# Layer 0's decay matrices by scans on VectorE, with G in two PSUM banks and D times x added by VectorE

## The reference

```python
dt = softplus(zxbcdt[..., D_INNER + CONV_DIM:] + dt_bias)
dA = jnp.exp(dt * A)
dBx = jnp.einsum('blhp,bln,blh->blhpn', x, Bmat, dt)
def step(state, inp):
    dA_t, dBx_t = inp
    state = state * dA_t[:, :, None, None] + dBx_t
    return (state, state)
y = jnp.einsum('lbhpn,bln->blhp', states, Cmat)
y = y + D[None, None, :, None] * x
y = rmsnorm(y.reshape(B, L, D_INNER) * silu(z), norm_gate_w, eps=1e-05)
return y @ W_out
```

## Time and profile before

| | us |
|---|---|
| three runs | 1697.21, 1696.18, 1690.65 |
| median | 1696.18 |
| the profiled execution | 1692.49 |
| its span, from first to last instruction | 1690.8 |
| busy in the span: TensorE / VectorE / ScalarE / GpSimd | 1556.4 / 1122.5 / 768.9 / 706.8 |
| mean granted TensorE clock | 0.954 of 2.4 GHz |

### The profile page before, as it was taken

How to read it: one execution, slowest core, us unless ns; L and a number is a source line. 1 busy time by engine, 2 the same in 40 slices (tenths; PEclk the granted TensorE clock), 3 DMA queues, 4 the chain that set the end, 5 groups by cost and what they waited for, 6 DMA issues and landing times.

```text
span 1690.8 us, 23271 instructions
## 1 busy us (share of the span) xinstructions
PE 1556.4 (92%) x7307; PEld 1073.6 (63%) x7307; DVE 1122.5 (66%) x2583; ACT 768.9 (45%) x1562; POOL 706.8 (42%) x751
## 2 busy tenths in 40 slices
PE   4989999999999999999878888899988999999996
PEld 3555756757566575756554455555557888988985
DVE  4868577684866758576248888987875654555542
ACT  1425162451625425162316555566545555555562
POOL 1555536364563655536311222233232553443452
PEclk7979989999999999999889999999999999999998
DMA  6000020101001010010122111111102442433432
GB/s 200 0 13 13 1 63 1 50 12 38 25 0 59 4 50 12 0 51 1 38 88 90 35 63 62 60 58 52 50 25 85 102 100 65 85 74 86 96 51 25
DMA packets 66855, 84.00 MB, mean 50 GB/s; under 512 B 12360, under 2 KB 57296, under 8 KB 66768
## 3 DMA queue, kind: packets, MB, share of 16 engines
q1 hardware_dynamic: 54480, 65.86, 12.1%
q0 software_dynamic: 12288, 17.05, 6.0%
HBM read 57.53 MB, written 25.36 MB: 49 GB/s over the span
## 4 chain that ended last, share of the span: by engine, by line
PE 26%; issue 13%; POOL 7%; DVE 3%; ACT 1%; DMA 1%; PEldq 0%; POOLq 0%; DVEq 0%; PEld 0%; SPq 0%
PE bank L2060 25%; POOL yb L920 2%; POOL Xs L912 2%; POOL ry L928 1%; PE bank L2435 1%; DVE am L1874 1%; POOL out L976 1%; POOL ry L925 0%; POOL xg L951 0%; DVE hits L1780 0%; DVE E L1896 0%; DVE yb L1907 0%; DVE u L1874 0%; DMA xg<-rows_d,IDX 0%; DMA hT<-xnT_d 0%
## 5 line engine op out<-in xcount | busy, mean ns | idle before, releaser
L2015 DVE TENSOR_TENSOR aml<-m0big,amh 128x512 fp32r<-128x512 f32 x128 | 88.0, 688 | 175.4 <-ACT amh L1320 175.3
L976 POOL DMA_INDIRECT out<-EW,IDX x64 | 105.1, 1642 | 223.5 <-DVE EW L2000 208.9
L1315 ACT ACTIVATE m0big<-bank,eb 128x512 f32<-128x512 f32 x128 | 87.9, 687 | 161.3 <-PE bank L2060 145.9
L2060 PE MATMUL bank<-w2h,amh 128*128 128x256 f32 x512 | 147.9, 289 | 0.0
L2060 PE MATMUL bank<-h2T,EW 128*128 128x512 f32 x320 | 146.8, 596 | 0.3
L2060 PE MATMUL bank<-w2h,aml 128*128 128x256 f32 x512 | 144.8, 283 | 0.0
L2060 PE MATMUL bank<-w2l,amh 128*128 128x256 f32 x512 | 144.7, 283 | 0.0
L2060 PEld LDWEIGHTS bank<-Xdt,E 128*128 128x128 f32 x768 | 95.7, 201 | 56.7 <-issue 56.7
L2060 PE MATMUL bank<-EW,am 128*128 128x256 f32 x512 | 115.8, 379 | 1.2 <-DVE am L1639 1.2
L920 POOL TENSOR_TENSOR yb<-yb,zs 128x512 f32<-128x512 f32 x32 | 40.5, 1267 | 171.9 <-DVE yb L1911 171.8
L1110 ACT ACTIVATE am<-bank,b 128x512 f32<-128x512 f32 x64 | 43.9, 686 | 148.0 <-PE bank L2060 148.0
(11 more groups left out here) (327 smaller groups left out, 3810.0 us busy)
## 6 DMA issues: line engine op xcount, KB each, us to landing
EW<-in_e_w SPq DMA_DIRECT2D x16, 1024.0 KB, 5.5
m0big<-dA_d SPq DMA_DIRECT2D x16, 512.0 KB, 4.7
xin<-in_L_attn_x SPq DMA_DIRECT2D x8, 512.0 KB
xp<-in_L_attn_x SPq DMA_DIRECT2D x8, 512.0 KB, 3.7
rows_d<-xo SPq DMA_DIRECT2D x8, 512.0 KB, 3.0
x_d<-xb SPq DMA_DIRECT2D x8, 512.0 KB, 4.0
xnT_d<-nT SPq DMA_DIRECT2D x8, 512.0 KB, 4.4
out<-x SPq DMA_DIRECT2D x32, 128.0 KB, 1.7
```

Of the source, the lines that this page charges most:

```text
L976: g.indirect_dma_start(out=out_rows, out_offset=bass.IndirectOffsetOnAxis(ap=IDX[:, 4 * u + c:4 * u + c + 1], axis=0), in_=ye[:, q, c, :], ...
L1315: a.activation(am2[:, j % 2, :], bank[j % 2][:, :], ACT.Gelu, bias=eb1[:, u // 2, j:j + 1]).then_inc(gelu_sig.sem, 1)
L2015: v.tensor_tensor(aml[:, j % 4, :], am2[:, j % 2, :], amh[:, j % 4, :], ALU.subtract).then_inc(am_low.sem, 1)
L2060: return t.matmul(out_, lhsT, rhs, start=first, stop=last)
```

## The change

It concerns layer 0 alone. R, its two sums on TensorE per chunk, ScalarE's exps of them and the mask product Gm are removed. In their place:

- TensorE transposes the log decays of the step (LOGT, 32 rows: four chunks of eight heads), behind the decay sums, and both now stand behind the input projections. ScalarE takes the exp into dAT0, whose first column is zero.
- SP stores dAT0 to DRAM and loads it back broadcast to 128 partitions, one transfer of 512 KB per chunk, into four buffers E0 (two new ones and the two halves of E). SP's loop over the steps is written out.
- VectorE scans each buffer in place in two halves against four identities side by side (ID0, in the room of b2), `scans`. The scans of chunks 0 and 1 stand around `chunk(0)`, those of chunk c+2 behind `sums(c)` and `mixed0(c-1)`.
- G and B's transposes go to two banks in turn, MISC and the former SEG; VectorE multiplies the scanned decays with G straight from PSUM.
- VectorE adds XD to yb in `sums`, in place of GpSimd in `gated`; GpSimd's XD waits for the sum two chunks back.

```diff
-        R = sb("R", [P, 8 * P])
+        dA0b = sb("dA0b", [P, 8 * P])
+        dAT0 = sb("dAT0", [CH * 8, P])
...
+        E0 = (dA0a[:, :], dA0b[:, :], E[:, 0, :], E[:, 1, :])
...
+        LOGT = MISC[0:CH * 8, 384:512]
+        GP0 = (MISC[:, 128:256], SEG[:, 128:256])
+        BTP0 = (MISC[:, 256:320], SEG[:, 256:320])
+        ID0 = b2[:, :, :].rearrange("p a n -> p (a n)")
...
+            def store_decays(i):
+                sp.wait_ge(own, 2)
+                s0.dA.wait_ge(sp, i, 1)
+                for c in range(CH):
+                    s0.dA_loaded[c].wait_ge(sp, i, 0)
+                sp.dma_start(dA0_d.rearrange("c (h t) -> (c h) t", t=P), dAT0[:, :]).then_inc(s0.dA_stored.sem, 16)
+            def load_decays0(i, c):
+                if c == 0:
+                    s0.dA_stored.wait_ge(sp, i, 16)
+                s0.intra_full.wait_ge(sp, i - 1, c + 1)
+                sp.dma_start(E0[c], dA0_d[c].partition_broadcast(P)).then_inc(s0.dA_loaded[c].sem, 16)
+            def decays_of(i):
+                store_decays(i)
+                load_decays0(i, 0)
+                load_decays0(i, 1)
+            def later_decays_of(i):
+                load_decays0(i, 2)
+                load_decays0(i, 3)
...
-            with sp.Fori(1, STEPS - 2) as b:
+            for b in range(1, STEPS - 2):
                 load_x(b + 2)
+                decays_of(b + 1)
                 load_residual(b + 1)
+                later_decays_of(b + 1)
                 store_back(b)
...
-            def terms(L, s, i, c, ch):
-                s.a.wait_ge(pool, i, 1)
-                s.seg_full.wait_ge(pool, i, c * L.segs)
-                nh = L.heads
-                v = R[:, 0:nh * P].rearrange("p (h t) -> p h t", h=nh)
-                a = s.dtv_buf[:, 1, c * nh:(c + 1) * nh].unsqueeze(2).to_broadcast([P, nh, P])
-                g.tensor_tensor(v, triU[:, :].unsqueeze(1).to_broadcast([P, nh, P]), a,
-                                ALU.mult).then_inc(s.R.sem, 1)
...
+                s.y0.wait_ge(pool, i, c - 1)
...
                 s.y0.wait_ge(pool, i, c + 1)
-                s.xd.wait_ge(pool, i, c + 1)
-                ch.put(g.tensor_tensor(yb[:, q, :], yb[:, q, :], XD[:, q, :], ALU.add))
-                ch.see(pool)
                 s.zs.wait_ge(pool, i, c + 1)
                 g.tensor_tensor(yb[:, q, :], yb[:, q, :], zs[:, q, :], ALU.mult).then_inc(s.yg.sem, 1)
...
-                if f is not None:
-                    terms(L, s, f, 0, pool0)
                 if b is not None:
                     back_rms(b, CH - 1, CH, poolb)
                     h2_sig.wait_ge(pool, b, CH)
...
-                    terms(L, s, f, 1, pool0)
                     xrows(L, s, f, 0)
                     xrows(L, s, f, 1)
                     for c in range(CH):
-                        if c + 2 < CH:
-                            terms(L, s, f, c + 2, pool0)
                         gated(L, s, f, c, pool0)
...
                 s.cum_full.wait_ge(act, i, 1)
                 a.activation(s.ex_buf[:, :, 0:n], CUM.rearrange("p (j n) -> p j n", j=3)[:, :, 0:n],
                              ACT.Exp).then_inc(s.ex.sem, 1)
+                s.dA_stored.wait_ge(act, i, 0)
+                a.activation(dAT0[:, 1:P], LOGT[:, 1:P], ACT.Exp).then_inc(s.dA.sem, 1)
...
                     if j == 0:
                         raw(L, s, i, 4)
+                        decay_exp(L, s, i)
...
-                def decays(j):
-                    s.seg_full.wait_ge(act, i, c * L.segs + j + 1)
-                    a.activation(E[:, q, 512 * j:512 * (j + 1)], SEG[:, :], ACT.Exp).then_inc(s.E.sem, 1)
-                s.intra_full.wait_ge(act, i, c - 1)
-                decays(0)
                 p = front_wait(act, L, s, i, f"xt{c}")
                 s.xdt.wait_ge(act, i, c - 1)
                 s.xd.wait_ge(act, i, c - 1)
                 a.activation(Xsb[:, q, :], p[:, :], ACT.Copy).then_inc(s.xsb.sem, 1)
-                for j in range(1, L.segs):
-                    decays(j)
...
                 if f is not None:
-                    decay_exp(L, s, f)
                     chunk(L, s, f, 0)
...
-                v.tensor_tensor(Gm[:, q, :], GP, triU[:, :], ALU.mult).then_inc(s.gm.sem, 1)
...
-                v.tensor_copy(Bs[:, q, 0:L.state], BTP[:, 0:L.state]).then_inc(s.bs.sem, 1)
+                v.tensor_copy(Bs[:, q, 0:L.state], BTP0[q][:, 0:L.state]).then_inc(s.bs.sem, 1)
                 s.xsb.wait_ge(dve, i, c + 1)
-                s.intra_full.wait_ge(dve, i, c - 1)
                 v.tensor_tensor(Xdt[:, q, :].rearrange("p (h e) -> p h e", h=nh),
                                 Xsb[:, q, :].rearrange("p (h e) -> p h e", h=nh),
                                 s.dtv_buf[:, 0, c * nh:(c + 1) * nh].unsqueeze(2).to_broadcast([P, nh, hp]),
                                 ALU.mult).then_inc(s.xdt.sem, 1)
-                s.gm.wait_ge(dve, i, c + 1)
                 for j in range(L.segs):
                     s.E.wait_ge(dve, i, c * L.segs + j + 1)
-                    e3 = E[:, q, 512 * j:512 * (j + 1)].rearrange("p (h t) -> p h t", h=4)
-                    v.tensor_tensor(e3, e3, Gm[:, q, :].unsqueeze(1).to_broadcast([P, 4, P]),
-                                    ALU.mult).then_inc(s.M.sem, 1)
+                    e3 = E0[c][:, 512 * j:512 * (j + 1)].rearrange("p (h t) -> p h t", h=4)
+                    v.tensor_tensor(e3, e3, GP0[q].unsqueeze(1).to_broadcast([P, 4, P]), ALU.mult).then_inc(s.M.sem, 1)
+            def scans(L, s, i, c):
+                s.dA_loaded[c].wait_ge(dve, i, 16)
+                for j in range(L.segs):
+                    e = E0[c][:, 512 * j:512 * (j + 1)]
+                    v.tensor_tensor_scan(e, e, ID0, 0.0, ALU.mult, ALU.add).then_inc(s.E.sem, 1)
...
                 ch.put(v.tensor_tensor(s3, s3, ex3[0:n, 2, :].unsqueeze(2).to_broadcast([n, nh, hp]), ALU.mult))
                 s.t1.wait_ge(dve, i, c + 1)
+                s.xd.wait_ge(dve, i, c + 1)
+                ch.put(v.tensor_tensor(yb[:, q, :], yb[:, q, :], XD[:, q, :], ALU.add))
+                ch.see(dve)
                 s.intra_full.wait_ge(dve, i, c + 1)
                 v.tensor_tensor(yb[:, q, :], yb[:, q, :], INTRA[:, :], ALU.add).then_inc(s.y0.sem, 1)
                 p = front_wait(dve, L, s, i, f"state{c}")
-                ch.see(dve)
                 v.tensor_tensor(S[:, :], S[:, :], p[0:n, :], ALU.add).then_inc(s.S.sem, 1)
...
                 if f is not None:
                     start(L, s, f)
+                    scans(L, s, f, 0)
                     chunk(L, s, f, 0, dve0)
+                    scans(L, s, f, 1)
                 for c in range(CH):
...
                         sums(L, s, f, c, dve0)
                         if c:
                             mixed0(s, f, c - 1)
+                        if c + 2 < CH:
+                            scans(L, s, f, c + 2)
...
+            v.tensor_copy(ID0.rearrange("p (h t) -> p h t", h=4),
+                          ident[:, :].unsqueeze(1).to_broadcast([P, 4, P])).then_inc(own, 1)
+            v.memset(dAT0[:, 0:1], 0.0).then_inc(own, 1)
+            dve.wait_ge(own, 2)
             norm(0)
...
                 s.a.wait_ge(pe, i, 1)
-                s.bs.wait_ge(pe, i, 0)
+                s.M.wait_ge(pe, i, 0)
                 m = CH * L.heads
                 for j, mat in enumerate((triU, strL, ones)):
-                    last = mm(CUM[:, 32 * j:32 * j + m], mat[:, :], s.dtv_buf[:, 1, 0:m])
+                    mm(CUM[:, 32 * j:32 * j + m], mat[:, :], s.dtv_buf[:, 1, 0:m])
+                last = t.transpose(LOGT, s.dtv_buf[:, 1, 0:m], ident[:, :])
                 last.then_inc(s.cum_full.sem, 1)
...
                 for j in range(1, 5):
                     in_proj(L, s, i, j)
+                decay_log_sums(L, s, i)
                 for part in between[2:]:
...
-                def decay_sums(j):
-                    s.E.wait_ge(pe, i, c * L.segs + j)
-                    mm(SEG[:, :], strL[:, :], R[:, 512 * j:512 * (j + 1)]).then_inc(s.seg_full.sem, 1)
-                s.R.wait_ge(pe, i, c + 1)
-                decay_sums(0)
...
-                s.bs.wait_ge(pe, i, c)
+                if c >= 2:
+                    s.M.wait_ge(pe, i, (c - 1) * L.segs)
                 if c == 0:
-                    s.ex.wait_ge(pe, i, 1)
...
-                mm(GP, s.u_buf[0:n, 4, cols(c)], s.Ct_buf[0:n, cols(c)])
-                t.transpose(BTP[:, 0:n], s.u_buf[0:n, 4, cols(c)], ident[0:n, 0:n]).then_inc(s.g_full.sem, 1)
-                for j in range(1, L.segs):
-                    decay_sums(j)
+                    s.dA.wait_ge(pe, i, 1)
+                mm(GP0[q], s.u_buf[0:n, 4, cols(c)], s.Ct_buf[0:n, cols(c)])
+                t.transpose(BTP0[q][:, 0:n], s.u_buf[0:n, 4, cols(c)], ident[0:n, 0:n]).then_inc(s.g_full.sem, 1)
...
-                    last = mm(INTRA[:, j * hp:(j + 1) * hp], E[:, q, j * P:(j + 1) * P],
```

(2 more changed lines are left out.)

33 lines of the change are left out of this document (17 added, 16 removed).

## The result

Median 1713.8 us (1708.0 to 1715.9, four runs) against 1696.7 (1690.7 to 1697.5, four runs of the kernel before): ratio 1.010, 95% interval 1.009 to 1.012. The profiled execution took 1712.7 us, its span is 1710.6, its mean granted clock 0.924 instead of 0.954. The forecast was +7.6 us and 1700, range 1664 to 1724, with slower by over 0.5% the likeliest sign at 0.40; the profiled executions differ by 20.2. One run further down, 1746.2 us of the last order with SBUF, was in a slower state of the chip and is left out of that kernel's time.

What follows compares the result with a forecast made beforehand. TensorE's own work was taken as the bound. A step 0.9 us longer, 6.3 in seven, plus 0.5 in step 0 and 0.75 at the start, made 7.6 on the profiled 1692.49: 1700 us, range 1664 to 1724.

Steps and rivals of the forecast that it cites:

- What goes: TensorE loses two strL x R products per chunk, 1.83 us, 7.3 per step; one transpose, 0.15 at most, is added.
- the DMA cover: Decays' store and broadcast load land at 441 to 443, wanted at 449; costed at nothing.
- The head: Ahead of z0, moving the decay sums delays up projections 0.45 us and frees as much; z0 starts where it did.
- The place that decides: Chunk 0's inter product waits for VectorE's zs(1) and starts at 458.9; TensorE stands idle 5.5 us.
- Blocking: GpSimd operations hold up VectorE's two-input work ahead of zs(1): bounds 0 and 4 times 1.04, taken as 1.7 us.
- The clock: Half clock behind the gap ahead of inter(0), in chunk 0's inter, state and intra products: 2.6 us lost.
- The rest of the chain: From y0(0) on: y0(1) at 475.6, y0(2) at 486.5, down projections at 496.6 against 495.74.
- the signs of being right: TensorE idle 4 to 6 us ahead of inter(0), clock near 0.5 behind; later short waits ended by zs.
- the forecast's own range: Gap ahead of inter(0), half clock, nearly all won back later: 1700, from 1686 to 1714, chance 0.38.
- the slower rival: Half clock through recurrence, up and z; each chunk's scans lose a whole GpSimd operation: 1710 to 1728, chance 0.26.
- The mild gap: GpSimd blocks little, zs(1) at 457.2, and the clock loses 1.7: 1680, from 1666 to 1688, chance 0.26.

Runs made afterwards that it cites:

- the last order with SBUF: Changed kernel with zs ahead of the scans in all chunks, scans of chunk 0 early, identities in SBUF: 1722.9 us, ratio 1.015.
- the kernel with both moves: Changed kernel with chunk 0's scans between the MLP's up operations and zs of chunk 1 ahead of its scans: 1708.0 us, ratio 1.007.
- filled wait: Changed kernel with four more 128x512 products on TensorE ahead of chunk 0's inter product in every layer 0 step: 1688.1 us, ratio 0.9965.
- the fastest kernel: Changed kernel with zs ahead of the scans in chunks 1 to 3, scans of chunk 0 early, identities in PSUM: 1650.5 us, ratio 0.972.
- zs ahead of the scans: Changed kernel with VectorE making zs ahead of the chunk's two scans for chunks 0 and 1: 1704.1 us, ratio 1.004.

## Why the prediction was right, and where not

The time lay in the range, and part of its nearness is luck. In layer 0 the change cost 11.7 us where 7.6 were forecast, and that small difference is made of larger ones: about 11 too little for the clock, 6 not foreseen as a gain of the head and 1 in step 0. The other 8.1 lay where no term was.

**What goes.** Right in size (z(0) to xt(0), from which one product of R went, took 2.66 and takes 1.72; forecast 0.86 less), and the DMA cover held: the store was issued at 438.63, the loads at 440.04 and 440.44, and no scan waited for one. **The head** was wrong by a microsecond: "z0 starts where it did" set 0.45 of delay against as much gain. The sums came to stand in TensorE's 0.97 us wait for h2T. From the down projections to the next z(0) it was 51.90 us in the mean before and is 50.95; with the log sums alone moved it is 50.92.

**The place that decides.** Right: inter(0) behind zs(1), in every step, at z0+12.0 (forecast +12.6). Missed: z(1) waits for zs(0) too, as it uses z0's bank, 0.9 to 1.04 us; the forecast had TensorE done with chunk 1's preparation at 453.4, z0+7.1, and it was at z0+8.5. The idle time of 5.5 us came as 1.04 and 3.46, together 4.5. **Blocking**: 1.7 us were taken; no scan was blocked, only up(4) (1.47 instead of 0.6) and Xdt a little, 1.0 in all. Where VectorE's two-input operations follow each other it was GpSimd that waited, and the forecast had no price for that side. In the changed kernel it hid behind the half clock; in the kernel with both moves TensorE waited for it.

**The clock** is the term that was mis-sized. Taken: 5.2 us at half clock, 2.6 lost, ended within chunk 0. In step 4 it reached to the end of up(5) and cost 3.4 us against the later chunks' rows (0.5 in state, 1.7 in intra, 1.2 in up). In step 5 it began with inter(0) and ended within z(2), 12 us: 0.9, 0.9, 1.7, 1.85 and 0.7, together 6.1. Step 4 is the mildest of the seven (inter(0) to inter(1) 12.31; the others 13.75 to 15.15; before 10.69). With the forecast's terms for the rest, xt to inter(3) would have been 42.9; step 4 has 42.87, and its down projections start at z0+50.26, which is the forecast to the last digit, by luck: in the other six it is z0+51.42 to 53.11. The mean from xt to inter(3) is 44.48: 1.6 us per step more, 11 in seven steps, of which the head returned 6.

**The rest of the chain** held: in step 4 y0(1) is done at z0+29.5 (forecast +29.3) and y0(2) at +40.7 (+40.2). Ahead of the later inter products TensorE waits 0.69 to 0.78 us, once in a step and on zs, as the signs of being right had it. E x G takes 0.6, start to start.

**Behind layer 0** 8.1 us were lost in code that is the same in both kernels; the forecast had no term for it. Over the fourteen kernels of this study the time from inter(3) of step 7 to the end is 897.7 (before), 898.4 (filled wait) and 899.9 (the fastest kernel) to 905.8 (after) and 910.4 (the last order with SBUF). In the kernel after the granted clock is lower at some places: in ten us of layer 1 that begin 110 us behind that inter(3), 0.50 against 0.79, and at the start of the experts, 490 us behind it, 0.66 against 1.00. At others it is higher, 1.00 against 0.76 at 430 us. Part of this falls anew with each execution: ten runs of the kernel with the filled wait took 1684.6 to 1695.4 us at a mean clock of 0.947 to 0.940. How much of the 8.1 is owed to the changed layer 0, no run here tells.

**Rivals.** 1713.8 lies at the upper end of the forecast's own range (1686 to 1714) and within the slower rival's, 1710 to 1728, and half of that rival's mechanism came with it: half clock through the recurrence, up and, in most steps, z. Its other half, scans that lose a whole operation of GpSimd in each chunk, didn't come in the changed kernel; where Xs began with them two scans took 3.13 us instead of 2.33 (zs ahead of the scans, both moves, the last order with SBUF). The mild gap had the blocking right and the clock wrong, and its time was added up wrongly: 1.8 us less per step than the forecast is 12.6 below the forecast's 1700, which gives 1687.5, not 1680. The kernel with the filled wait, with chunk 0 at full clock, took 1688.1.

## What to carry to other kernels

A wait of the engine that sets the pace cost its length here and then, mostly, the clock behind it. Filling it with useless products gave back 19 us in layer 0 and 26 in all. So when a change adds a wait of a few microseconds, price what lies behind it at half clock over some 9 to 12 us, not over one chunk. When work moves to another engine, ask first what stands behind it in that engine's order: the same parts gave 1714 us with the long operation ahead of the one that opens the next bank, and 1650 behind it. That took one more thing: the identities, which every scan of VectorE reads beside a busy GpSimd, had to be in PSUM, without which the same order gave 1723.
